# Both of a step's attention-value portions stand in one run at the head of the next step

## The chip, the cores and the metric

The kernel runs on one core of one Trainium2 chip. Its time is the device time of one launch in microseconds (us), lower is better, and the median of several runs counts. One execution was also recorded by the hardware profiler. The engines are PE (TensorE, matrix products), ACT (ScalarE), DVE (VectorE), POOL (GpSimd) and SP (which issues transfers); each works through its own program in order, and they wait for each other by semaphores.

## The reference

Two transformer layers on x of shape (8, 512, 128), float32. Cut to what matters:

```python
x = x + L0_attn(layernorm(x))    # 16 heads of width 8; q and k scaled to unit length,
                                 # out = softmax(g_scale * q k^T) v
x = x + L0_ffn(layernorm(x))     # top 1 of 8 experts, width 32, gelu
x = x + L1_attn(layernorm(x))    # 16 heads of width 64, causal softmax, then w_o
x = L1_ffn(layernorm(x))         # top 2 of 8 experts, width 512, gelu, then layer norm
```

The change concerns the product of the first attention, softmax(...) v, alone; everything it computes stays as it is.

## The kernel before, in words

The work of the eight batches is laid over one long loop of passes `i` from -3 to 8, each of eight steps `p` from 0 to 7 (`steps`). In a pass the stages stand side by side, each for another batch: the second attention of batch i, which works on one pair of heads per step (`o.pair(0)`), the first attention of batch i + 2, the small layers between them (batches i + 1 and i + 3), and the routing of batch i - 1. The dense second expert layer follows after the loop. What follows is about the loop.

The first attention of a batch is cut into 16 portions, one for each group of four heads and each block of 128 keys, and a step has two of them, `o.cosine(0)` and `o.cosine(1)`. For each portion PE computes the scores (`cosines`, L1662, four products of 32 x 128), ACT takes their exponential into one of two buffers (`cosine_exp`, L824, two instructions of 128x1024), and PE multiplies the result with the values (`values0`, L1675, four products that each fill 16 columns). The second attention has, for its pair, score products in three units (`score_unit`, L1529), score products for the maximum in three units for the next pair (`max_unit`, L1498; DVE takes the maxima, L1085), projections of the pair after that (`project`, L1469), the sums (L1559, L1561), the transposed maxima (L1509) and the products with the values (`values1`, L1548).

All score units, of both attentions, alternate between two banks of PSUM, the tile `scores`: a unit may be opened only when the unit two before it has been taken out by ACT or DVE (`unit_open`). In a step the units come as pair 0, max 0, the two halves of portion 0, pair 1, max 1, pair 2, max 2, and the two halves of portion 1; then the next step's pair 0, for which the bank of the first half of portion 1 must be free. The many smaller results alternate in the same way between the two banks of the tile `work` (`work_open`, `work_moved`), in the order that `work_order` writes down.

PE's program is written out by hand at the end of the tensor block: the head of a step is `score_unit(o.g, 0)`, `max_unit(..., 0)`, `values0` and the first half of `values1`, then `cosines` of portion 0. Near the end of a step stands `cosines` of portion 1 and behind it the tail, which depends on p: nothing at p = 0; `group_operands` (L1648, eight transposes into two banks of `work`) at p = 1, 3, 5 and 7; besides that `projection_out` (L1578) at p = 1 and p = 6, `values1_rows` (L1469) at p = 3, the transposes of L1476 at p = 5, `logits0` and `hidden0` (L1596, L1605) at p = 2, and `experts0_out` and `qkv0` (L1637, L1638, L1588) at p = 4. Portions and pairs run together in the six passes i = 0 to 5; in the two passes before them the first attention runs without pairs, and behind them it is over.

Of the kernel before, what the change touches and what calls it, by code (L numbers as in the profile page):

```python
# [217 lines left out]
def layers_kernel(nc, x, wqkv0, g_scale, wg0, s0, bias_ln0, w1_0, b1_0, w2_0, b2_0,  # L218
# [3 lines left out]
    with ctx:  # L222
# [101 lines left out]
        def vstat(h):  # L324
            n = TILES * H0 * VCOLS
            return a0_part(VSTAT + (h % 2) * n, n).rearrange("p (t h d) -> p t h d", t=TILES, h=H0)

        def prob0(c):
            return a0_part(PROB0 + (c % PROB0_SLOTS) * HG * SEQ, HG * SEQ)
# [207 lines left out]
        def unit_done(eng, *unit):  # L537
            eng.wait_ge(score_free[UNIT_NO[unit] % 2], unit_fills(*unit) + 1)
# [915 lines left out]
        def _(pe):  # L1454
# [34 lines left out]
            def max_unit(g, i):  # L1489

                if i == 0:
                    pe.wait_ge(qk1_hi, 2 * g + 2)
                d = unit_open(pe, "max", g, i)
                tiles = (((3, 0),), ((2, 0), (0, 3 * P)), ((1, 0),))[i]
                for n, (qt, at) in enumerate(tiles):
                    width = (qt + 1) * P
                    for j in range(2):
                        last = mm(d[:, j * SEQ + at:j * SEQ + at + width],  # L1498
                                  q_hi[heads(j), g % 2, qt * P:(qt + 1) * P],
                                  k_hi[heads(j), g % 2, 0:width], start=(n == 0),  # L1500
                                  stop=(n == len(tiles) - 1))
                last.then_inc(unit_full("max", g, i), 1)
# [148 lines left out]
            def cosines(c):  # L1651

                s, g, kb = c // STEPS0, c % STEPS0 // TILES, c % TILES
                if kb == 0:
                    work_moved(pe, "qT", s, g)
                    work_moved(pe, "kT", s, g)
                for half in range(2):
                    d = unit_open(pe, "cosine", c, half)
                    for i in range(2):
                        j = 2 * half + i  # L1660
                        rows = slice(STRIP * j, STRIP * (j + 1))
                        last = mm(d[:, i * SEQ:(i + 1) * SEQ],  # L1662
                                  qkT0[rows, 1, g % 2, kb * P:(kb + 1) * P],
                                  qkT0[rows, 0, g % 2, :], start=True, stop=True)
                    last.then_inc(unit_full("cosine", c, half), 1)

            def values0(c):

                s, g, kb = c // STEPS0, c % STEPS0 // TILES, c % TILES
                if kb == 0:  # L1670
                    pe.wait_ge(out_free[1], s * GROUPS0 + g + 1)
                unit_done(pe, "cosine", c, 0)
                unit_done(pe, "cosine", c, 1)
                for j in range(HG):
                    last = mm(outs[STRIP * j:STRIP * j + VCOLS, 1, :],  # L1675
                              vstat(s)[:, kb, g * HG + j, :], prob0(c)[:, j * SEQ:(j + 1) * SEQ],
                              start=(kb == 0), stop=(kb == TILES - 1))
                last.then_inc(out_full[1] if kb == TILES - 1 else pv0_done, 1)
# [34 lines left out]
            for o in steps():  # L1713
# [2 lines left out]
                    score_unit(o.g, 0)  # L1716
                if o.pair(1) is not None:
                    max_unit(o.pair(1), 0)
                if o.cosine(-1) is not None:
                    values0(o.cosine(-1))  # L1720
                if o.pair(-1) is not None:
                    values1(o.pair(-1), (0, 1))
                if o.cosine(0) is not None:
# [67 lines left out]
                    project("k", 1, o.pair(2))  # L1791
                if o.cosine(1) is not None:
                    cosines(o.cosine(1))
                if o.cosine(0) is not None:
                    values0(o.cosine(0))

                if p in (1, 3, 5) and s is not None:
                    group_operands(s, p // 2 + 1)
# [132 lines left out]
```

## Time and profile before

| | us |
|---|---|
| median of 3 runs | 1633.49 |
| lowest, highest run | 1622.28, 1648.9 |
| the profiled execution, its own time | 1636.53 |
| its span, first to last instruction | 1634.8 |
| PE busy | 1327.0 (81%) |
| DVE busy | 934.6 (57%) |
| ACT busy | 851.8 (52%) |
| POOL busy | 600.4 (37%) |
| `values0` on PE (L1675) | 148.4 busy, 1024 records |
| mean granted TensorE clock | 0.917 of full |

The profile page lists busy time by engine, the span in 40 slices, the chain of waits that ended last, and groups of instructions by source line. PE records a float32 product as two instructions, so that the four products of one portion's `values0` are eight records. The timeline lists instructions in order of time, merged where they follow each other from one line; what is in brackets is the engine's idle time before and what ended it. The clock that the throttle granted has two levels in this trace, full (2.4 GHz) and half (1.2 GHz).

### The profile page before, as it was taken

What the parts mean: (1) busy time and instruction counts of PE and PEld (TensorE: products, weight loads), DVE (VectorE), ACT (ScalarE), POOL (GpSimd) and SP (SyncE); (2) the same over time, 40 slices, a digit from 0 to 9 for tenths busy, and PEclk for the clock granted to TensorE, in tenths of its full rate; (3) what the DMA queues carried; (4) which work ended last, traced back from release to release, by engine and by line L of the source; (5) the groups of instructions that cost most, each with busy time, mean ns of one, the idle gap of its engine ahead of it and who ended that gap; (6) DMA issues with size and microseconds to landing.
All of it is one profiled execution on the core that took longest, in us unless ns stands there. A gap on an engine that the chain in (4) does not pass through costs nothing.

```text
span 1634.8 us, 27815 instructions
## 1 busy us (share of the span) xinstructions
PE 1327.0 (81%) x9189; PEld 798.3 (49%) x9189; DVE 934.6 (57%) x3262; ACT 851.8 (52%) x1642; POOL 600.4 (37%) x768
## 2 busy tenths in 40 slices
PE   3878888988888789889988988988888884599970
PEld 1223444554455445545445444544555553488860
DVE  5355755565756576656555764555554654265655
ACT  3665665656565556555654665444424531255533
POOL 1010322233253335333423442235325444265554
PEclk7878999999999999989998999899979987699985
DMA  7060990000000000000000000001010000212222
GB/s 288 1 229 1 8 3 1 1 7 8 1 14 8 7 1 21 1 7 3 19 1 8 8 8 1 7 8 59 8 43 36 1 11 22 90 54 55 58 90 104
DMA packets 63051, 53.17 MB, mean 33 GB/s; under 512 B 39752, under 2 KB 49488, under 8 KB 62656
## 3 DMA queue, kind: packets, MB, share of 16 engines
q1 hardware_dynamic: 58592, 42.47, 13.2%
q0 software_dynamic: 4320, 8.92, 1.6%
q8 instruction: 78, 1.28, 0.3%
q14 instruction: 61, 0.50, 0.1%
HBM read 20.56 MB, written 30.81 MB: 31 GB/s over the span
## 4 chain that ended last, share of the span: by engine, by line
PE 59%; DVE 17%; ACT 14%; issue 7%; POOL 2%; DMA 1%; POOLq 1%; SPq 0%; DVEq 0%; ACTq 0%
PE scores L1529 10%; PE work L1469 8%; PE outs L1675 7%; PE outs L1548 6%; DVE scores L1085 5%; ACT a_buf L824 5%; PE work L1578 4%; PE scores L1498 3%; DVE ra L1078 3%; PE scores L1662 3%; PE work L1561 3%; ACT ra L830 3%; PE outs L1860 2%; ACT rsum L836 2%; PE work L1559 2%
## 5 line engine op out<-in xcount | busy, mean ns | idle before, releaser
L1085 DVE CUSTOM_DVE_ANT_0 scores<-scores,mask_qk 128x512 f32<-128x512 f32 (+3 forms) x512 | 239.3, 520 | 240.8 <-PE scores L1498 238.1
L824 ACT ACTIVATE a_buf<-scores 128x1024 f32<-128x1024 f32 x256 | 248.0, 1026 | 110.7 <-PE scores L1662 101.4
L676 POOL TENSOR_SCALAR_AFFINE_SELECT big<-big 128x256 f32<-128x256 f32 x256 | 100.9, 407 | 541.5 <-ACT big L818 540.7
L818 ACT ACTIVATE big<-scores 128x1024 f32<-128x1024 f32 (+1 forms) x192 | 169.2, 882 | 231.0 <-PE scores L1529 224.5
L1529 PE MATMUL scores<-ra 64*128 64x512 f32 (+3 forms) x1536 | 188.8, 352 | 47.2 <-ACT a_buf L824 33.0
L686 POOL TENSOR_TENSOR big<-big 128x768 f32<-128x768 f32 x64 | 118.6, 1854 | 191.2 <-PE work L1561 191.0
L1529 PEld LDWEIGHTS scores<-ra 64*128 64x128 f32 x1536 | 124.4, 193 | 109.4 <-ACT a_buf L824 42.3
L1548 PE MATMUL outs<-big 128*64 128x512 f32 (+3 forms) x1024 | 164.8, 449 | 2.2 <-DVE yT L1109 2.2
L1675 PE MATMUL outs<-a_buf 128*16 128x512 f32 x1024 | 148.4, 655 | 8.6 <-DVE wqkv_lo L1032 4.9
L1109 DVE TENSOR_TENSOR yT<-outs,rsum 128x512 f32<-128x512 f32 x64 | 44.3, 692 | 148.4 <-ACT rsum L841 148.4
L1548 PEld LDWEIGHTS outs<-big 128*64 128x64 f32 x1024 | 64.2, 137 | 115.9 <-issue 103.4
L973 ACT ACTIVATE big<-scores,b_sb 128x128 f32<-128x128 f32 x284 | 81.1, 368 | 74.8 <-PE scores L1850 43.5
L669 POOL TENSOR_TENSOR rstd<-var_eps,minus_half 128x4 f32<-128x4 f32 x48 | 50.5, 1052 | 161.9 <-DVE var_eps L1047 161.9
L830 ACT CAST ra<-work 128x512 fp32r<-128x512 f32 x128 | 75.0, 586 | 61.7 <-PE work L1469 59.3
L773 POOL DMA_INDIRECT choice_rows<-big x71 | 69.7, 982 | 81.6 <-DVE big L1410 79.7
L1078 DVE TENSOR_TENSOR ra<-work,ra 128x512 fp32r<-128x512 f32 x128 | 87.9, 687 | 18.1 <-ACT ra L830 12.7
L1498 PE MATMUL scores<-ra 64*128 64x512 f32 (+3 forms) x512 | 81.6, 355 | 14.1 <-DVE neg_max L1085 13.1
L836 ACT ACTIVATE rsum<-work 128x512 f32<-128x512 f32 x64 | 38.2, 597 | 101.7 <-PE work L1561 101.7
L1529 PE MATMUL scores<-neg_max_T,pick 64*128 64x512 f32 (+3 forms) x512 | 85.7, 329 | 0.0
L1662 PE MATMUL scores<-qkT 32*128 32x512 f32 x512 | 74.3, 516 | 12.8 <-ACT a_buf L824 10.5
L689 POOL TENSOR_TENSOR big<-big 128x512 f32<-128x512 f32 x64 | 82.4, 1288 | 5.0
L1469 PE MATMUL work<-x_hi,wqkv_hi 128*128 128x512 f32 x128 | 67.7, 529 | 20.0 <-ACT rsum L836 19.8
(216 smaller groups left out, 2600.7 us busy)
## 6 DMA issues: line engine op xcount, KB each, us to landing
sorted_rows<-xrows SPq DMA_DIRECT2D x33, 520.0 KB, 6.8
big<-sorted_rows SPq DMA_DIRECT2D x71, 65.0 KB
a_buf<-in_w SPq DMA_DIRECT2D x2, 2048.0 KB, 8.2
a_buf<-choice_rows SPq DMA_DIRECT2D x16, 256.0 KB, 4.9
a_buf<-in_x SPq DMA_DIRECT2D x8, 256.0 KB, 2.9
x_rows<-x SPq DMA_DIRECT2D x8, 256.0 KB, 2.0
ra<-x_rows SPq DMA_DIRECT2D x8, 256.0 KB
out<-a_buf SPq DMA_DIRECT2D x8, 256.0 KB, 2.0
```

The lines of the kernel that those rows point to most:

```text
L686: nc.gpsimd.tensor_tensor(tsum, prob1(g, 0)[:, :, P:SEQ], prob1(g, 1)[:, :, 0:3 * P], ALU.add).then_inc(tsum_step, 1)
L818: activation(prob1(g, i), d[:, :, 0:256] if i == 2 else d, ACT.Exp, scale=SCALE1).then_inc(unit_free("pair", g, i), 1)
L824: activation(prob0(c)[:, i * 1024:(i + 1) * 1024], unit_wait(act, "cosine", c, i), ACT.Exp).then_inc(unit_free("cosine", c, i), 1)
L830: copy(dst[:, g % 2, :], w).then_inc(qk1_hi, 1)
L1078: v.tensor_tensor(lo[:, g % 2, :], w, hi[:, g % 2, :].bitcast(F32), ALU.subtract).then_inc(free_of(which, g), 1)
L1085: return v.tensor_tensor_reduce(scores_, scores_, mask_qk[:, SEQ - width:SEQ], -1.0, 3e38, ALU.add, ALU.min, neg_max[:, qt, j:j + 1])
L1469: last = mm(dst, a, c, start=(n == 0), stop=(n == 2))
L1498: last = mm(d[:, j * SEQ + at:j * SEQ + at + width], q_hi[heads(j), g % 2, qt * P:(qt + 1) * P], k_hi[heads(j), g % 2, 0:width], start=(n ...
L1529: last = mm(d[:, j * SEQ + at:j * SEQ + at + width], lhs, c[heads(j), g % 2, queries], start=(n == 0 and term == 0), stop=(n == len(blocks ...
L1548: last = mm(outs[heads(j), 0, kb * P:], v1[:, kb, n * D1:(n + 1) * D1], probs, start=(kb == 0), stop=(kb == TILES - 1))
L1662: last = mm(d[:, i * SEQ:(i + 1) * SEQ], qkT0[rows, 1, g % 2, kb * P:(kb + 1) * P], qkT0[rows, 0, g % 2, :], start=True, stop=True)
L1675: last = mm(outs[STRIP * j:STRIP * j + VCOLS, 1, :], vstat(s)[:, kb, g * HG + j, :], prob0(c)[:, j * SEQ:(j + 1) * SEQ], start=(kb == 0), ...
```

## The change

PE's program alone is written differently. Before, portion 0 of a step was multiplied with its values near the end of the same step, behind `cosines` of portion 1, and portion 1 at the head of the next step. Now both stand at the head of the next step, one behind the other. No instruction is added or taken away, and DVE, ACT, POOL and SP have the same programs as before.

```diff
                     score_unit(o.g, 0)
                 if o.pair(1) is not None:
                     max_unit(o.pair(1), 0)
-                if o.cosine(-1) is not None:
-                    values0(o.cosine(-1))
+                for n in (-2, -1):
+                    if o.cosine(n) is not None:
+                        values0(o.cosine(n))
                 if o.pair(-1) is not None:
                     values1(o.pair(-1), (0, 1))
                 if o.cosine(0) is not None:
...
                 if o.cosine(1) is not None:
                     cosines(o.cosine(1))
-                if o.cosine(0) is not None:
-                    values0(o.cosine(0))
 
                 if p in (1, 3, 5) and s is not None:
                     group_operands(s, p // 2 + 1)
```

The first place is PE at the seam between steps p = 0 and p = 1, where a step has no tail. `qkT` are the operands of the first attention, `a_buf` holds its exponentials and values, `ra` the operands of the second attention and `big` its exponentials. Before:

```order
L1469 MATMUL work<-x_hi,wqkv_lo 128x512
L1662 MATMUL scores<-qkT 128x512 x4
L1675 MATMUL outs<-a_buf 16x512 x4
L1529 MATMUL scores<-ra 128x512 x6
L1529 MATMUL scores<-neg_max_T,pick 128x512 x2
L1498 MATMUL scores<-ra 128x512 x2
L1675 MATMUL outs<-a_buf 16x512 x4
L1548 MATMUL outs<-big 64x512 x2
L1548 MATMUL outs<-big 64x384 x2
L1662 MATMUL scores<-qkT 128x512 x4
```

And with the change:

```order
L1469 MATMUL work<-x_hi,wqkv_lo 128x512
L1662 MATMUL scores<-qkT 128x512 x4
L1529 MATMUL scores<-ra 128x512 x6
L1529 MATMUL scores<-neg_max_T,pick 128x512 x2
L1498 MATMUL scores<-ra 128x512 x2
L1675 MATMUL outs<-a_buf 16x512 x8
L1548 MATMUL outs<-big 64x512 x2
L1548 MATMUL outs<-big 64x384 x2
L1662 MATMUL scores<-qkT 128x512 x4
```

The four products that stood between portion 1's scores and the next pair's scores stand behind the maximum's scores now, in one run with the four that were there.

The second place is PE at the seam between p = 4 and p = 5, where the first layer's experts are the tail. The difference, with its context:

```order
 L1662 MATMUL scores<-qkT0 128x512 x4
-L1675 MATMUL outs<-a0_buf 16x512 x4
 L1637 MATMUL work<-w2_0_sb,a0_buf 128x128 x2
 L1638 MATMUL work<-b2_0_sb,a0_buf 128x128
```

```order
 L1529 MATMUL scores<-neg_max_T,pick 128x512 x2
 L1498 MATMUL scores<-ra 128x512 x2
-L1675 MATMUL outs<-a0_buf 16x512 x4
+L1675 MATMUL outs<-a0_buf 16x512 x8
 L1548 MATMUL outs<-big 64x512 x2
```

The tail follows the scores of portion 1 directly, and the head has the run of eight. The seams at the other steps differ in the same way.

## Rows read from the trace of the kernel before

**Rows 1.** The profile page: busy time by engine, the granted clock in 40 slices, the chain.

```profile
PE 1327.0 (81%) x9189; PEld 798.3 (49%) x9189; DVE 934.6 (57%) x3262; ACT 851.8 (52%) x1642; POOL 600.4 (37%) x768
...
PEclk7878999999999999989998999899979987699985
...
PE 59%; DVE 17%; ACT 14%; issue 7%; POOL 2%; DMA 1%; POOLq 1%; SPq 0%; DVEq 0%; ACTq 0%
```

**Rows 2.** Timeline of PE, two projections: start, us, engine, line, tiles [idle before].

```profile
801.39 0.50 PE L1469 MATMUL work<-x_hi,wqkv_hi 128*128 128x512 f32 x1
...
802.19 0.40 PE L1469 MATMUL work<-wqkv_hi,x_hi 128*128 128x512 f32 x1
```

**Rows 3.** Timeline of PE, seam from p = 0 to p = 1.

```profile
806.87 1.05 PE L1675 MATMUL outs<-a_buf 128*16 128x512 f32 x8
808.19 0.98 PE L1529 MATMUL scores<-ra 64*128 64x512 f32 x6 [0.27 <-ACT a_buf L824]
...
809.57 1.05 PE L1675 MATMUL outs<-a_buf 128*16 128x512 f32 x8
810.55 1.73 PE L1548 MATMUL outs<-big 128*64 128x512 f32 x8
812.20 0.50 PE L1662 MATMUL scores<-qkT 32*128 32x512 f32 x4
```

**Rows 4.** Timeline of ACT, the same seam.

```profile
807.02 1.95 ACT L824 ACTIVATE a_buf<-scores 128x1024 f32<-128x1024 f32 x2
```

**Rows 5.** Timeline of PE, seam from p = 1 to p = 2.

```profile
825.29 3.84 PE L1578 MATMUL work<-wo_sb,yT 128*128 128x128 f32 x32 [0.45 <-DVE qkT L1131]
```

**Rows 6.** Timeline of DVE, the same seam.

```profile
823.32 0.68 DVE L1078 TENSOR_TENSOR ra<-work,ra 128x512 fp32r<-128x512 f32 x1
824.54 1.29 DVE L1131 CAST qkT<-work 128x512 fp32r<-128x512 f32 x2 [0.55 <-PE work L1648]
```

**Rows 7.** Timeline of PE, tail of p = 2 and middle of p = 3.

```profile
846.40 1.96 PE L1605 MATMUL work<-a_buf,w1s 128*128 128x512 f32 x4
...
856.67 0.80 PE L1529 MATMUL scores<-ra 64*128 64x384 f32 x6 [3.07 <-ACT a_buf L824]
```

**Rows 8.** Timeline of DVE, tail of p = 2.

```profile
844.84 0.68 DVE L1078 TENSOR_TENSOR ra<-work,ra 128x512 fp32r<-128x512 f32 x1
```

**Rows 9.** Timeline of ACT, step p = 3.

```profile
851.73 1.28 ACT L877 ACT_TABLE_LOAD   x1
...
855.60 1.94 ACT L824 ACTIVATE a_buf<-scores 128x1024 f32<-128x1024 f32 x2
```

**Rows 10.** Timeline of PE, the end of p = 4's tail.

```profile
895.40 1.34 PE L1588 MATMUL work<-wqkv_sb,a_buf 128*128 128x384 f32 x2 [0.26 <-DVE res L1332]
```

**Rows 11.** Timeline of DVE, the same place.

```profile
894.84 0.76 DVE L1332 TENSOR_TENSOR res<-res,work 128x256 f32<-128x256 f32 x2
```

**Rows 12.** Timeline of PE, heads behind the tails of p = 6 and p = 7.

```profile
935.86 0.96 PE L1529 MATMUL scores<-ra 64*128 64x512 f32 x6
...
952.42 0.96 PE L1529 MATMUL scores<-ra 64*128 64x512 f32 x6
```

**Rows 13.** Timeline of DVE, tail of p = 7.

```profile
950.97 0.68 DVE L1078 TENSOR_TENSOR ra<-work,ra 128x512 fp32r<-128x512 f32 x1
```

**Rows 14.** Stretches behind p = 3's long wait: us, busy by engine, clock, DMA.

```profile
227.00:235.00 8.00, 7.33 (x40) 5.50 (x40) 3.07 (x15) 3.83 (x6) 2.16 (x4) 0.59 1.49 2
384.00:392.00 8.00, 6.94 (x52) 5.23 (x48) 4.29 (x17) 3.70 (x6) 2.16 (x4) 0.81 0.00 1
857.00:869.00 12.00, 11.21 (x63) 7.17 (x59) 5.68 (x25) 5.63 (x10) 4.11 (x6) 0.57 0.00 1
```

**Rows 15.** A longer and a shorter wait of PE, in the timeline.

```profile
180.14 0.38 PE L1509 MATMUL work<-ident_b,neg_max_hl 128*128 128x128 bf16 x4 [3.00 <-DVE ra L1078]
...
1044.85 1.03 PE L1694 MATMUL work<-wg_sb,xnT 128*128 128x8 f32 x8 [1.37 <-DVE ra L1078]
```

**Rows 16.** The stretch behind the shorter one, columns as in rows 14.

```profile
1045.00:1050.00 5.00, 4.85 (x27) 2.83 (x27) 0.94 (x3) 1.83 (x4) 2.08 (x2) 0.66 0.00 0
```

## The prediction

> **What bounds the kernel.** I read the page first: PE is busy for 81% of the span, no other engine above 57%, the chain of waits lies on PE for 59% and on DVE and ACT for 31%, and the granted clock is near full in the loop's middle but not everywhere [rows 1]. So PE's own program sets the time, together with the short waits at which it is released by ACT or DVE. The change touches PE's order alone. I therefore went through PE's timeline for the whole pass i = 3 (about 785 to 950 us; it repeats six times with a period of 156 to 160 us), and at each of its eight seams looked at ACT and DVE for what would release PE if it came earlier. A moved instruction costs its time at the new place and gives it back at the old one only if what stands behind it can start earlier; that is the question at each seam.
>
> **The price at the head.** One portion of `values0` takes 0.98 us at full clock: one starts at 809.57 and `values1` behind it at 810.55 [rows 3]. At the head the moved portion joins one that is there already. The first product after another kind of tile lasts longer than one that follows its own kind: a projection's first product has 0.50 us, the first of the next projection, directly behind, 0.40 [rows 2], so 0.1 us more. Before, the portion stood alone between two other kinds; in a run with its twin one such transition falls away, whereas the tail keeps its own. I take 0.87 us for the addition at the head (0.98 less 0.11). The bounds: 0.98 if a run saves nothing, and 0.5 if the two portions' fixed parts merged entirely, for which no row speaks. Nothing absorbs it there: `cosines` starts at 812.20 directly behind `values1`, with no wait [rows 3], and the later waits in the step count from PE's own instructions and move along.
>
> **What comes back at the old place**, seam by seam, for a full pass.
>
> - p = 0, no tail: PE waits already, 0.27 us, for ACT's exponential of the first half, and starts the pair's scores at 808.19 [rows 3]. ACT runs from 807.02 to 808.97 for two halves [rows 4]; the first ends there at 808.0, and no earlier portion of PE changes that. The cover of 0.98 us turns into idle time, 0.27 becomes about 1.25. Returned: 0. Net +0.87.
> - p = 1, 3, 5: the tail is `group_operands`. Its second half needs the `work` bank of `k`, which DVE frees at 824.00 (823.32 + 0.68), and what stands behind waits for DVE's copy that now starts at 824.54 [rows 5, 6]. Without `values0` the first half is done long before 824.00, DVE goes over to the copy at 824.00 at once, 0.54 us earlier, and I count 0.49. Net +0.38, three times: +1.14.
> - p = 2: the hidden layer starts at 846.40 [rows 7] and could start when DVE has freed `k`'s bank, at 845.52 [rows 8]: 0.9 us earlier, and with it the next pair's scores and ACT's exponential of them. In p = 3 PE then waits 3.07 us for ACT, which between loads two tables for the gelu and starts the portion's exponentials at 855.60 [rows 7, 9]. ACT's sequence begins 0.9 us earlier, whereas PE reaches its wait at the same time as before: here the 0.87 at the head costs nothing, since the wait covers it. The wait falls to about 2.2. Net -0.9.
> - p = 4: the tail ends in `qkv0`, which waits 0.26 us until DVE has taken out the experts' first result. DVE does that from 894.84 on [rows 10, 11], at the end of an unbroken row of routing instructions (L1062 to L1209) that doesn't depend on the tail. Returned: 0, the wait becomes 1.2. Net +0.87 in the four passes with both routing and `qkv0`, -0.11 in the first and the last, where one of them is missing.
> - p = 6: the output projection needs nothing that is late, and the head behind it starts without a wait at 935.86 [rows 12]. All of 0.98 returns. Net -0.11.
> - p = 7: as p = 1, with the head directly behind the transposes at 952.42; DVE frees the bank at 951.65 [rows 12, 13], four transposes (0.44) follow, so 952.09. Returned 0.33. Net +0.54.
>
> Sum of a full pass: 0.87 + 1.14 - 0.9 + 0.87 - 0.11 + 0.54 = +2.4 us. Four such passes give 9.6. Pass 0 has 1.6 (p = 1 has no projection behind its transposes, so it goes as p = 7; p = 4 at -0.11). Pass 5 has 2.2 (p = 4 at -0.11; at p = 5 and p = 7 nothing returns, for DVE is late there or the tail is empty). Together **+13.4 us**. In the two passes without pairs the order hardly changes (the portions stood side by side already, with the transposes between them at most), and there ACT's exponentials bind: 0. The part after the loop is untouched.
>
> **The clock.** Behind each of the six waits of 3.07 us the granted clock falls to half for a while: means of 0.59, 0.81 and 0.57 in stretches of 8, 8 and 12 us [rows 14]; two more passes look like the second and one like the third. At half the clock PE does half its work, so a stretch costs its length times the missing share, 3.3, 1.5 and 5.2 us; over the six passes 3.3 + 3 x 1.5 + 2 x 5.2 = 18.2, 3.0 each. With 2.2 us, the wait lies between these (of the same length one, 3.00, kept the clock) and those of 1.0 to 1.5, most of which kept it; but one, 1.37 [rows 15], has 0.66 over the 5 us behind it [rows 16], 1.7 us. I take half of the six as saved: -9.1. Against it stand ten new waits of about 1.2 us, at p = 0 and p = 4, close behind others; I count one drop, +3. Clock: -6.
>
> The Trainium skill (TensorE: Matmul & The Clock Gate, "Why this matters for your kernels") says that long idle gaps between bursts of matmuls send the clock back to its lower rate, and that shorter ones don't. If 2.2 us counts as short in its sense, all 18.2 come back, which is the first rival below; the trace's 3.00 us without a drop shows that the length alone doesn't decide.
>
> **Sum:** 13.4 - 6 = +7 us. Against the profiled execution, 1636.5, that is 1643.5. The median of the runs shown is 3 us lower, so I predict a median of **1640 us**, +0.4%.
>
> **The rivals.**
>
> 1. The clock stays up behind all of p = 3's waits: 13.4 - 18.2 = -5, 1629 us. For it: the wait loses almost a third. Against it: the fall came behind all six so far, whatever the phase, and one came behind 1.37 us. 0.18.
> 2. The dependences alone count, since PE's clock falls as often as before: +13.4, or +19 if the run saves no transition (48 x 0.11 more): 1647 to 1652. For it: no row shows a run of two at full clock. 0.22.
> 3. Slower beyond a doubt: the new waits at p = 0 and p = 4 lose the clock. The place is the head behind them, the price 3.0 us, the mean of the six above. For it: each of the new waits stands some us behind PE's usual short ones, as the 1.37 us did which lost it. Against it: most waits of this length kept the clock. All ten: +30, with the 13.4 together +43, 1677. It passes 2% from seven drops on, with none saved at p = 3. 0.11.
> 4. The run of two is much cheaper than its parts, or PE's tails start so much earlier that ACT and DVE get ahead for good. To pass 2%, 33 us over 48 seams, each would have to bring 0.7 us, and with the 13.4 of dependences 1.0, all that a portion costs. Nothing in the profile says so: 1595. 0.05.
>
> My forecast has the remaining 0.44.
>
> **Range and chances.** Forecast, rivals 1 and 2 hold 0.84 between 1629 and 1652; the median of three runs before lay within 1622 to 1649, so it may be off by some us by itself. 1624 to 1660 holds that and part of rival 3. 2%, 33 us, is about what a measurement of this kernel can tell from no change. Faster by over 2%, below 1601: rival 4, 0.05. Slower by over 2%, above 1666: rival 3, 0.11, with 0.01 for what I haven't seen. Within 2%: 0.83.
>
> **What would show it.** Right: at p = 0's seam PE waits 1.2 to 1.3 us before the pair's scores, for ACT's L824, six times; in p = 3 the wait is 2.1 to 2.3 instead of 3.07; at p = 4 PE waits about 1.2 us before L1588 for DVE; a run of 16 records of L1675 takes 1.8 to 1.9 us from its start to `values1`; a pass without a fall of the clock is about 2.4 us longer. PE's busy time falls by up to 5 us at equal clock. Wrong: if at p = 1, 3 and 5 the full 0.98 us returns, the sum loses 3 x 6 x 0.49 = 9 us and the change is neutral or better; if the tail of p = 2 does not start earlier, 0.9 x 6 = 5 us are added and all of the clock's return is lost; if the clock's mean in the loop falls, rival 3.

## The result, and the profile after

The changed kernel takes 1661.24 us (median of 4 runs, 1656.16 to 1668.99); the kernel before, in the same set, 1640.13. The ratio is 1.021, with an interval from 1.012 to 1.030: slower, by 1 to 3%. Every ratio in this document is taken over the runs of its set that count as fast, here only two of the four of the kernel before, whereas medians, means and clocks are over all runs, so that the two medians alone give 1.013. I had forecast 1640. A second set of runs of the same change gave 1.011 (1.007 to 1.015). Over all sets the mean is 1661 us for the ten runs of the change and 1641 for the 84 runs of the kernel before, so +20 us, 1.2%. The 1633.49 that the prediction started from, a median of three runs, was 8 us lower than that mean.

The profiled execution has 1660.31 us, span 1658.6. The page of after, busy time, clock and chain [rows 1]:

```profile
PE 1332.8 (80%) x9189; PEld 807.1 (49%) x9189; DVE 940.0 (57%) x3262; ACT 852.1 (51%) x1642; POOL 600.0 (36%) x768
...
PEclk7878999999999989998999999989989987699995
...
PE 53%; DVE 18%; ACT 15%; issue 9%; POOL 3%; POOLq 1%; DMA 1%; SPq 0%; DVEq 0%; ACTq 0%
```

PE's share of the chain falls from 59% to 53%, and its busy time is 6 us longer with the same 9189 instructions: the work got neither more nor less, but parts of it ran at half clock, and PE waits more. Its waits sum to 270.8 us instead of 254.2. The six passes i = 0 to 5 (from the first scores of p = 0 to those of the pass behind) take 972.9 us instead of 945.2; what comes ahead is 2.7 us shorter and what comes behind 1.1.

**The seams are as predicted.** The timeline of PE of after, p = 0's seam in pass 3 [rows 3]:

```profile
828.78 0.51 PE L1662 MATMUL scores<-qkT 32*128 32x512 f32 x4
830.55 1.20 PE L1529 MATMUL scores<-ra 64*128 64x512 f32 x6 [1.26 <-ACT a_buf L824]
...
832.53 2.87 PE L1675 MATMUL outs<-a_buf 128*16 128x512 f32 x16
835.33 1.73 PE L1548 MATMUL outs<-big 128*64 128x512 f32 x8
```

The wait went from 0.27 to 1.26 us. But the scores behind it take 1.20 and the run of two portions 2.87: the clock fell here. The same view from p = 1's tail, and from the end of p = 2's tail to the wait in p = 3 [rows 5, 7]:

```profile
848.84 0.53 PE L1648 MATMUL work<-ident_r,parts 128*128 128x128 f32 x4 [0.54 <-DVE ra L1078]
...
870.66 1.96 PE L1605 MATMUL work<-a_buf,w1s 128*128 128x512 f32 x4
...
873.91 1.91 PE L1675 MATMUL outs<-a_buf 128*16 128x512 f32 x16
875.75 1.73 PE L1548 MATMUL outs<-big 128*64 128x512 f32 x8
...
880.93 0.79 PE L1529 MATMUL scores<-ra 64*128 64x384 f32 x6 [2.22 <-ACT a_buf L824]
```

The bank of `k` costs 0.54 us where the portion used to cover it; at full clock the run of two takes 1.84 us to the start of `values1`, which is 2 x 0.98 less 0.12; the long wait is 2.22 instead of 3.07.

**The new cost is in the clock at p = 4.** Steps p = 4 and p = 5 of the passes 1 to 4, one window each, in the kernel before (columns as in [rows 14]):

```profile
397.49:439.78 42.29, 36.59 (x267) 20.51 (x266) 26.00 (x98) 23.00 (x43) 13.29 (x19) 1.00 0.02 8
554.35:596.68 42.33, 36.57 (x267) 20.47 (x266) 26.01 (x99) 23.00 (x43) 13.27 (x19) 1.00 0.02 7
711.23:755.97 44.74, 39.43 (x268) 21.73 (x268) 25.76 (x99) 23.14 (x43) 13.28 (x19) 0.92 0.02 7
872.46:916.32 43.86, 38.10 (x267) 21.11 (x266) 25.33 (x98) 23.00 (x43) 12.27 (x16) 0.96 0.02 7
```

And after:

```profile
399.50:445.45 45.95, 39.46 (x268) 22.09 (x268) 26.36 (x98) 23.04 (x43) 13.83 (x20) 0.93 0.02 7
562.72:612.08 49.36, 43.88 (x267) 24.66 (x266) 26.00 (x99) 23.15 (x43) 13.91 (x20) 0.83 0.02 6
727.67:777.00 49.33, 43.88 (x267) 25.21 (x266) 26.17 (x99) 23.14 (x43) 13.82 (x20) 0.83 0.02 6
894.14:939.96 45.82, 39.50 (x267) 21.74 (x266) 25.99 (x99) 23.05 (x43) 13.91 (x20) 0.93 0.02 7
```

Read the second number of a row (its length) with the clock: 42.3 us at full clock before, and up to 49.4 at 0.83 after; none of the four is at full clock. The sum is 190.5 us instead of 173.2, so +17.2, of which about 1 us per pass is order. Pass 2 of the kernel before has the portion ahead of the tail's small products, all at full clock:

```profile
571.75 1.05 PE L1675 MATMUL outs<-a_buf 128*16 128x512 f32 x8
572.73 0.71 PE L1637 MATMUL work<-w_sb,a_buf 128*128 128x128 f32 x4
573.37 0.48 PE L1638 MATMUL work<-b_sb,a_buf 8*128 8x128 f32 x2
...
577.27 0.89 PE L1588 MATMUL work<-wqkv_sb,a_buf 128*128 128x384 f32 x2 [0.25 <-DVE res L1332]
578.09 0.96 PE L1529 MATMUL scores<-ra 64*128 64x512 f32 x6
```

In pass 2 of after the clock falls ahead of the tail, behind a wait that both kernels have, and this runs at half clock:

```profile
576.91 1.03 PE L1694 MATMUL work<-wg_sb,xnT 128*128 128x8 f32 x8 [1.25 <-DVE ra L1078]
...
579.95 0.79 PE L1469 MATMUL work<-x_hi,wqkv_hi 128*128 128x512 f32 x1
...
582.25 1.22 PE L1637 MATMUL work<-w_sb,a_buf 128*128 128x128 f32 x4
583.40 0.79 PE L1638 MATMUL work<-b_sb,a_buf 8*128 8x128 f32 x2
...
589.75 1.65 PE L1588 MATMUL work<-wqkv_sb,a_buf 128*128 128x384 f32 x2
591.33 1.65 PE L1529 MATMUL scores<-ra 64*128 64x512 f32 x6
...
593.75 2.79 PE L1675 MATMUL outs<-a_buf 128*16 128x512 f32 x16
596.47 1.73 PE L1548 MATMUL outs<-big 128*64 128x512 f32 x8
```

and in pass 4 the same tail at full clock, with the new wait at its end [rows 10]:

```profile
916.79 0.71 PE L1637 MATMUL work<-w_sb,a_buf 128*128 128x128 f32 x4
917.43 0.48 PE L1638 MATMUL work<-b_sb,a_buf 8*128 8x128 f32 x2
918.77 0.89 PE L1588 MATMUL work<-wqkv_sb,a_buf 128*128 128x384 f32 x2 [0.85 <-DVE res L1332]
919.59 1.44 PE L1529 MATMUL scores<-ra 64*128 64x512 f32 x6
```

There are two forms of the loss. In pass 2 the clock was down before the tail, and it stays down through the tail's small products and the next head. In pass 4 the clock was up in the tail, PE waits 0.85 us for DVE, and it falls directly behind. Where the clock was up through all of the step, the new wait has the length that I had forecast; so in pass 3 of e6_p4 (below, moved at p = 4 only), and there too the clock falls in the head behind it:

```profile
744.99 0.89 PE L1588 MATMUL work<-wqkv_sb,a_buf 128*128 128x384 f32 x2 [1.24 <-DVE res L1332]
745.80 1.58 PE L1529 MATMUL scores<-ra 64*128 64x512 f32 x6
```

### The profile page after: what moved, and what is told of

Same layout as the page of the kernel before. It is cut to its first block, busy times and chain, and to the rows that moved or that the text cites. A ratio compares the mean times of both kernels' runs of the same rounds, so it can differ in the third digit from the quotient of the medians.

```text
span 1658.6 us, 27816 instructions
## 1 busy us (share of the span) xinstructions
PE 1332.8 (80%) x9189; PEld 807.1 (49%) x9189; DVE 940.0 (57%) x3262; ACT 852.1 (51%) x1642; POOL 600.0 (36%) x768
## 4 chain that ended last, share of the span: by engine, by line
PE 53%; DVE 18%; ACT 15%; issue 9%; POOL 3%; POOLq 1%; DMA 1%; SPq 0%; DVEq 0%; ACTq 0%
PE scores L1529 10%; PE work L1469 7%; PE outs L1675 7%; PE outs L1548 6%; DVE scores L1085 5%; ACT a_buf L824 5%; PE work L1578 4%; DVE ra L1078 4%; PE scores L1498 3%; PE work L1561 3%; ACT ra L830 3%; ACT rsum L836 2%; PE scores L1662 2%; PE work L1559 2%; PE outs L1859 1%
## 5 line engine op out<-in xcount | busy, mean ns | idle before, releaser
L1529 PE MATMUL scores<-ra 64*128 64x512 f32 (+3 forms) x1536 | 189.6, 353 | 49.0 <-ACT a_buf L824 36.0
L1529 PEld LDWEIGHTS scores<-ra 64*128 64x128 f32 x1536 | 123.5, 192 | 109.1 <-ACT a_buf L824 38.9
L1675 PE MATMUL outs<-a_buf 128*16 128x512 f32 x1024 | 140.9, 670 | 9.8 <-DVE wqkv_lo L1032 6.4
L1498 PE MATMUL scores<-ra 64*128 64x512 f32 (+3 forms) x512 | 82.2, 357 | 16.6 <-DVE neg_max L1085 13.4
L1529 PE MATMUL scores<-neg_max_T,pick 64*128 64x512 f32 (+3 forms) x512 | 86.4, 332 | 0.0
```

Of the source, the lines that this page charges most:

```text
L1498: last = mm(d[:, j * SEQ + at:j * SEQ + at + width], q_hi[heads(j), g % 2, qt * P:(qt + 1) * P], k_hi[heads(j), g % 2, 0:width], start=(n ...
L1529: last = mm(d[:, j * SEQ + at:j * SEQ + at + width], lhs, c[heads(j), g % 2, queries], start=(n == 0 and term == 0), stop=(n == len(blocks ...
L1675: last = mm(outs[STRIP * j:STRIP * j + VCOLS, 1, :], vstat(s)[:, kb, g * HG + j, :], prob0(c)[:, j * SEQ:(j + 1) * SEQ], start=(kb == 0), ...
```

## The experiments

Each kernel was timed in five rounds beside the kernel before. Run times scatter by 1% with the mean granted clock of the run, and do so within every kernel: a common line through the runs of all kernels has 12.1 us (11.3 to 12.9) for each 0.01 of the clock. So beside the ratio stands the difference from before at equal clock (what is left when each run is moved along that line to the mean clock of before), and the part that goes with the clock. The split is rough, as the clock that falls in a wait costs less than one that falls in work.

| kernel | moved at p | runs | median us | ratio (interval) | mean clock | at equal clock | with the clock |
|---|---|---|---|---|---|---|---|
| before | none | 84 | 1641.0 | 1 | 0.9153 | 0 | 0 |
| change, first set | all | 4 | 1661.2 | 1.021 (1.012 to 1.030) | 0.910 | +14.4 ± 2.9 | +6.4 |
| e5_whole | all | 6 | 1659.8 | 1.011 (1.007 to 1.015) | 0.910 | +13.4 ± 2.4 | +6.6 |
| e9_but4 | all but 4 | 8 | 1650.5 | 1.009 (1.005 to 1.012) | 0.918 | +12.9 ± 2.1 | -3.5 |
| e10_but04 | all but 0, 4 | 12 | 1645.0 | 1.006 (1.003 to 1.010) | 0.917 | +7.2 ± 1.8 | -1.7 |
| e3_odd | 1, 3, 5, 7 | 12 | 1647.1 | 1.004 (1.001 to 1.006) | 0.917 | +7.7 ± 1.8 | -1.5 |
| e2_p04 | 0, 4 | 6 | 1665.8 | 1.015 (1.011 to 1.018) | 0.904 | +9.0 ± 2.6 | +13.7 |
| e6_p4 | 4 | 12 | 1646.8 | 1.003 (1.000 to 1.007) | 0.911 | +1.0 ± 1.8 | +4.8 |
| e7_p0 | 0 | 12 | 1646.4 | 1.000 (0.997 to 1.003) | 0.915 | +3.6 ± 1.8 | +0.2 |
| e1_p26 | 2, 6 | 6 | 1624.8 | 0.988 (0.985 to 0.992) | 0.924 | -5.7 ± 2.5 | -10.5 |
| e12_p26 | 2, 6 | 12 | 1628.7 | 0.996 (0.992 to 0.999) | 0.922 | -3.3 ± 1.8 | -7.8 |
| e11_p2 | 2 | 12 | 1628.8 | 0.995 (0.992 to 0.998) | 0.924 | -2.2 ± 1.9 | -10.7 |
| e8_fill | 2, 6 and a fill | 12 | 1646.1 | 1.006 (1.003 to 1.009) | 0.908 | -3.6 ± 1.9 | +8.8 |
| e4_omit | none, two left out | 12 | 1644.9 | 0.997 (0.993 to 1.000) | 0.910 | -4.4 ± 1.8 | +6.6 |

A ratio is taken in its own set of runs; the last two columns use all sets.

**Only p = 2 and p = 6 moved** (e1_p26). The edit, which the other partial kernels share but for the numbers:

```diff
+                if (p - 1) % PAIRS in (2, 6) and o.cosine(-2) is not None:
+                    values0(o.cosine(-2))
                 if o.cosine(-1) is not None:
                     values0(o.cosine(-1))
...
-                if o.cosine(0) is not None:
+                if p not in (2, 6) and o.cosine(0) is not None:
                     values0(o.cosine(0))
```

> Portion 0 is moved to the next step's head only in steps p = 2 and p = 6; in all others it stays at its old place. Theory A (the waits of 1.2 us that the move opens at p = 0 and p = 4 lose the clock, and so does the bare tail of p = 4): the dependences give -0.6 us at p = 2 and 3 together (the wait of 3.07 us falls to 2.2, and the head costs nothing) and -0.12 at p = 6, so -5 us over six passes; the clock behind p = 3's wait falls for 1.7 us instead of 3.0 as in the full change, -5 more: 8 to 14 us faster than before, no new falls at p = 0 and p = 4. Rival B (the clock falls at random, whatever stands at the seams): the dependences alone, -5 us, with falls anywhere. Rival C (the run of two portions itself costs clock or time wherever it stands): 0 to +5 us, with falls behind the runs at p = 3 and p = 7.

Measured: 1624.8 us, 1.2% below the kernel before, and more than theory A had. Part of the change is a gain.

**Only p = 0 and p = 4** (e2_p04).

```diff
-in (2, 6)
+in (0, 4)
```

> The move is made only in steps p = 0 and p = 4. Theory A: dependences +0.85 at p = 0 in six passes and at p = 4 in four, +8.5 us; on top of it the clock, falls at about half of the p = 0 seams and in the middle or tail of most p = 4 steps, 10 to 20 us; and the full wait of 3.07 us at p = 3 stays, with its falls as before. Together 18 to 28 us slower than before, as much as the whole change. Rival B: +8.5 us and no more than by chance. Rival C: a third of what the whole change costs, +7 us, since a third of the runs of two is here, counting the pass-wise +24.

Measured: 1665.8 us, as slow as the whole change, with the lowest clock of all, 0.904. Theory A's 18 to 28 us hold.

**Only the odd steps** (e3_odd).

```diff
-in (2, 6)
+in (1, 3, 5, 7)
```

> The move is made only in steps p = 1, 3, 5 and 7. The seams of the changed kernel at full clock say +0.22 each at p = 1, 3 and 5 and +0.6 at p = 7, 1.3 us a pass, +8 us. Theory A: that, and clock falls as before: +5 to +10 us. Rival C: the runs of two lose the clock here as well, +15 us or more. Rival B: +8 us.

Measured: +7.7 us at equal clock, against 10.1 of the prediction's terms, and no effect on the clock.

**The portion left out** (e4_omit): the kernel before without the first portion's product at p = 0 and p = 4 of the six passes; it isn't done anywhere, so the sum is one portion short. A second edit, in `values0`, lets the portion behind it start the sum instead.

```diff
-                              start=(kb == 0), stop=(kb == TILES - 1))
+                              start=(kb == 0 or kb == 1 and left_out(c)),
+                              stop=(kb == TILES - 1))
...
-                if o.cosine(0) is not None:
+                if not (0 <= o.i <= 5 and p in (0, 4)) and o.cosine(0) is not None:
                     values0(o.cosine(0))
```

> The kernel before, but in the six passes with pairs the first portion's product with the values is left out in steps p = 0 and p = 4 (12 products of four; the output is wrong by them), and nothing is put in its place. Where it stood, PE waits 1.25 us for ACT at p = 0 and about 1 us for DVE at p = 4. By the dependences alone this changes nothing, 0 us (at p = 4 of the first and the last pass, without that wait, -1 us each). Theory A: the waits and the bare tail lose the clock as in the whole change, although there is less work: 8 to 18 us slower, with the seams at p = 0 and p = 4 as uneven as there. Rival B: -2 to 0 us.

Measured: 1644.9 us, no change, though 12 x 0.98 us of work are gone. Windows of steps p = 4 and p = 5 in its passes 2 and 3:

```profile
555.72:603.96 48.24, 42.93 (x259) 24.29 (x258) 25.75 (x99) 23.16 (x43) 13.32 (x19) 0.82 0.02 6
719.97:769.09 49.12, 44.03 (x261) 25.53 (x260) 25.74 (x99) 23.15 (x43) 13.29 (x19) 0.79 0.02 6
```

With less to do PE is busy for 44.0 us here; the kernel before has 36.6 in its passes at full clock. So the loss at p = 4 needs no run of two and nothing added at the head: it is enough that the portion is missing from the tail. (With the portion goes its cover of the wait for DVE, so the run does not tell the two apart.) That it would cost 8 us or more in all, as I expected in one case, did not come.

**The whole change again** (e5_whole), in another set of runs, with no edit to the changed kernel.

> The changed kernel as it is, timed again for more executions. Over 24 runs of the kernel before its time follows its mean granted clock, 12.4 us for each 0.01; by that line the four runs of the changed kernel stand 14 us above the kernel before at an equal clock, and 4 us more by a lower clock (0.910 against 0.913). Theory A': the dependences are 11 to 14 us (the three parts run so far sum to 5.4 less, 8.6 and 7.7 more, +11), and the clock falls by 0.003 to 0.006 in the mean, so 15 to 21 us slower. Rival: the clock part was chance, and at an equal clock only the dependences stay, 11 to 14.

Measured: 1659.8 us. The clock is again 0.910.

**Only p = 4** (e6_p4) **and only p = 0** (e7_p0).

```diff
-in (2, 6)
+in (4,)
```

> The move is made in step p = 4 only. Moving at p = 0 and p = 4 together gave +8.6 us at an equal clock and lowered the clock by 0.009, 12 us. Dependences here: +0.87 in four passes, -0.1 in two, +3.3 us. Theory D (the clock is lost at p = 4: the tail there is 8 products of 128 columns, and the portion of 512-column products that stood ahead of it is gone): the clock falls by 0.006 to 0.009, 7 to 11 us more, 10 to 14 together. Theory E (it is lost by the waits of 1.2 us, of which p = 0 has six and p = 4 four): 4 to 5 us by the clock, 8 together.

```diff
-in (2, 6)
+in (0,)
```

> The move is made in step p = 0 only. Dependences: +0.85 in six passes, +5.1 us. Theory D: the clock hardly changes, 0 to 3 us more, 5 to 8 together. Theory E: 7 us by the clock, 12 together.

Measured: 1646.8 and 1646.4 us, both within 0.4% of before by the ratios in their set. p = 4 alone lowers the clock by 0.004, p = 0 alone doesn't. That speaks against theory E; but p = 4's fall is smaller than the 0.006 to 0.009 of theory D. Windows of steps 4 and 5 of e6_p4, passes 1 and 3:

```profile
396.13:445.27 49.14, 43.83 (x268) 24.51 (x267) 25.84 (x98) 23.15 (x43) 13.21 (x19) 0.83 0.02 6
722.05:766.81 44.76, 37.98 (x267) 21.23 (x266) 25.96 (x99) 23.01 (x43) 13.31 (x19) 0.96 0.02 7
```

Its four passes are at 0.83, 0.86, 0.96 and 0.93. Both together (e2_p04) have more than the sum of the two, 22.7 us above the mean of before against 9.6; their clocks differ by more than p = 4's own part, and why is open.

**The wait of p = 3 filled** (e8_fill): e1_p26, with one block of `values1_rows` and the projection of q put ahead of the waiting scores of p = 3, from behind them.

Both stand no longer at their old places further on in the step (not shown):

```diff
+                if p == 3 and l1 is not None:
+                    values1_rows(l1, 2, 1)
+                if p == 3 and o.pair(2) is not None:
+                    project("q", 0, o.pair(2))
                 if o.pair(0) is not None:
                     score_unit(o.g, 1)
```

> The portion is moved at p = 2 and p = 6 only, as in the run that was 19 us faster; besides, in step p = 3 the projections of v (block 2) and of q, 0.7 us each, are issued ahead of the second pair unit instead of behind it, so that they fill the wait for ACT's gelu, which is 2.2 us there. Dependences: 1.5 us less in each of seven passes, -10 us against that run, -16 against the kernel before. If long waits of PE are what costs the clock, the mean clock rises above that run's 0.924, and it is 25 to 35 us faster than before. If it is not, 16 to 29.

Measured: 1646.1 us, 17 to 21 us above the two medians of what it was built on; both expectations missed. The timeline of PE, pass 1:

```profile
385.37 0.80 PE L1529 MATMUL scores<-ra 64*128 64x384 f32 x6 [0.63 <-ACT a_buf L824]
...
387.86 0.62 PE L1529 MATMUL scores<-ra 64*128 64x256 f32 x6 [0.83 <-ACT big L818]
...
391.31 0.59 PE L1613 MATMUL work<-ident_b,a_buf 128*8 128x128 bf16 x4 [1.58 <-DVE ra L1078]
...
396.81 1.91 PE L1675 MATMUL outs<-a_buf 128*16 128x512 f32 x8
```

The wait of 2.22 us is down to 0.63, and the clock stays up behind it. But the projection had covered two other waits: 0.83 us stands 2.5 us further on (not there in e1_p26, whose timeline has the scores directly behind the projection), and 1.58 where e1_p26 has 0.64. There the clock falls (the window 390 to 392 us has 0.62; in e1_p26 it fell between 386 and 388), and the portion at 396.81 has 1.91 us instead of 1.05. PE's waits sum to 252.8 us in the trace, 251.1 in e1_p26. The hole was moved, not filled; at equal clock the kernel is as fast as e1_p26, and its clock is lower by 0.015. What of this comes from where the waits now lie, I can't say.

**The change without p = 4** (e9_but4) **and without p = 0 and 4** (e10_but04).

```diff
-in (2, 6)
+in (0, 1, 2, 3, 5, 6, 7)
```

> The whole change, except that at p=4 the first portion stays where the kernel before has it. Theory A (the change costs what the order on TensorE costs, about 13.5 us at equal granted clock, of which p=4 is 5.2; and the granted clock falls behind the new wait of 0.85 us at p=4, which stretches the small products of that step's end): the sum at equal clock falls to about +8, the granted clock comes back to that of the kernel before (0.914), the stretch between p=4's tail and the next scores takes 9.1 us again in most passes instead of 11 to 15: 1645 to 1653. Theory B (the lower clock belongs to the moves together, by p=0's wait or by the longer runs of 16x512 products, not to p=4): the clock stays at 0.910 and p=4's stretch stays long: 1653 to 1658.

```diff
-in (2, 6)
+in (1, 2, 3, 5, 6, 7)
```

> The whole change except at p=0 and p=4: moved at p=1, 2, 3, 5, 6 and 7. By the terms of the prediction (+10.1 for the four odd steps, -6.1 for p=2 and 6) the order gives +4; by the parts timed so far +7.9 and -5.2, so +2.7, and the clock is that of the kernel before or a little above it, as 2 and 6 alone had 0.924: 1637 to 1648 (theory A). Theory B (all moves add up through the clock too: -17.3 for 2 and 6 and +5 for the odd ones as timed): 1630 to 1636. If neither holds and the steps' costs don't add, 1650 or more.

Measured: 1650.5 and 1645.0 us. Leaving p = 4 alone brings the clock from 0.910 back to 0.918 and takes 10 us off. The windows of steps 4 and 5 in e9_but4, passes 1 to 4:

```profile
397.72:440.22 42.50, 36.64 (x268) 20.63 (x268) 26.43 (x98) 23.02 (x43) 13.85 (x20) 1.00 0.02 7
558.36:600.91 42.55, 36.63 (x268) 20.63 (x267) 26.27 (x99) 23.02 (x43) 13.95 (x20) 1.00 0.02 7
719.04:762.82 43.78, 38.11 (x267) 20.89 (x267) 26.22 (x99) 23.11 (x43) 13.94 (x20) 0.96 0.02 7
879.61:923.39 43.78, 38.10 (x268) 21.00 (x268) 26.10 (x99) 23.11 (x43) 13.94 (x20) 0.96 0.02 7
```

The lengths of before are back, in a kernel that has every other portion moved: theory A's time and clock hold, theory B falls. e9_but4's part at equal clock, +12.9, is above the +8 expected; e10_but04's +7.2 is above the +2.7. The pieces do not add up to within their errors at equal clock, so single pieces of 1 to 4 us in that column aren't to be trusted further than that.

**Only p = 2** (e11_p2), **and p = 2 and 6 once more** (e12_p26).

```diff
-in (2, 6)
+in (2,)
```

> Moved at p=2 only. The wait of 3.07 us of step 3's head becomes 2.2 in six passes, so 6 x 0.98 = 5.9 less at equal clock, since the run of two saves 0.11 there too and the tail of p=2 hides nothing. Theory A (shorter wait, and with it a clock that stays up more often): 1626 to 1634. Theory B (2 and 6 alone had a high clock by chance or by p=6): 1634 to 1639. If the gain of 2 and 6 were p=6's alone: 1641 to 1645.

The last has no edit against e1_p26.

> The kernel moved at p=2 and 6 only, once more, in another set of runs. If its granted clock of 0.924 is its own: 1621 to 1629. If that clock was chance, and only the order gains (5.2 us at equal clock): 1633 to 1639.

Measured: 1628.8 and 1628.7 us. The high clock of e1_p26 is its own (0.922 in the second set), and it comes from p = 2. Windows of step 3 of e11_p2, passes 1, 2 and 3:

```profile
373.57:394.71 21.14, 16.89 (x130) 8.91 (x130) 12.84 (x50) 15.26 (x26) 7.50 (x9) 1.00 0.00 2
528.62:552.06 23.44, 19.67 (x130) 11.08 (x130) 12.85 (x50) 15.36 (x26) 7.54 (x9) 0.85 0.00 1
687.35:708.50 21.15, 16.90 (x131) 8.92 (x130) 12.85 (x50) 15.26 (x26) 7.51 (x9) 1.00 0.00 1
```

In three passes of six the clock does not fall at all behind the wait of 2.2 us. Over all kernels it fell behind each of the 36 waits of 3.07 us, and behind 32 of the 42 of 2.2: e11_p2 is, with e10_but04, the best of seven traces, not the typical one. Moving at p = 2 alone is the smallest edit that beats both kernels, the one before by 0.2 to 0.8%; p = 6 adds nothing that can be told.

## Why the prediction was wrong

**The order was right.** The length of each step at full clock, passes 1 to 4, from the starts of L1529 at the heads in the trace of after or, where none of its steps was at full clock, as noted:

| step | before | changed | measured | predicted |
|---|---|---|---|---|
| p = 0 | 16.12 | 16.98 | +0.86 | +0.87 |
| p = 1 | 20.87 | 21.08 | +0.21 | +0.38 |
| p = 2 | 19.23 | 19.35 | +0.12 | 0 |
| p = 3 (both at clock 0.92) | 22.25 | 21.58 | -0.67 | -0.49 |
| p = 4 (e9_but4, same head) | 23.72 | 24.56 | +0.84 | +0.87 |
| p = 5 (e5_whole) | 18.59 | 18.80 | +0.21 | +0.38 |
| p = 6 | 19.54 | 19.43 | -0.11 | -0.11 |
| p = 7 | 16.56 | 17.17 | +0.61 | +0.54 |

(The predicted column sorts the prediction's terms by the step in which they fall: the head gives +0.87 to every step but p = 3, where the wait covers it, and the tail gives back what the prediction says.) The sum is +2.1 us for a full pass instead of +2.4, so about +12 for the six instead of +13.4; the fits at equal clock have +13 to +14. p = 1, 3 and 5 give back 0.65 instead of 0.49, p = 2 0.75 instead of 0.87, p = 7 0.26 instead of 0.33. For p = 4's own portion e6_p4 and e2_p04 have the answer at full clock: step 4 as before (23.75), step 5 19.45 instead of 18.59, so 0.86 and nothing returned. The 0.11 us that a run of two saves is there. The Trainium skill (TensorEngine Tiling (Array Packing), "Tiling Modes") says that a change of tiling mode drains TensorE, without a figure; a run of 16-column products with one such change less shows 0.12, which agrees, though no run here shows that a drain is what it saves.

**The clock term failed: -6 predicted, +6 to +15 measured.** It had two parts, which I read again as missing clock (length times one less the granted clock, summed over the six passes; a microsecond missing in a wait costs nothing, so it is a bound on the time lost):

- Step 3. I counted half of 18.2 us as saved. The trace of after has 8.8 us missing there, before 18.8; but e5_whole, with the same program, has 15.4. Over the seven traces with p = 2 moved (e8_fill left aside) the mean is 13.6, over the six without 18.2. So a quarter comes back in the mean, not half; single traces spread so far (8.5 to 20.5 and 11.9 to 25.6) that the quarter itself is uncertain. The Trainium skill (TensorE: Matmul & The Clock Gate, "What's actually happening") says that the chip watches TensorE's activity in a rhythm of its own, which doesn't follow the program, so that the clock's changes can come at another place from one run to the next. The traces agree: with one and the same program, steps 4 and 5 of pass 3 took 49.3 us in the trace of after and 43.6 in that of e5_whole.
- The new waits. I counted ten of them as one fall, +3 us, and named more as rival 3, at a chance of 0.11. Steps 4 and 5 have 28.3 us missing after (e5_whole 26.3), before 7.8, and steps 0 to 2 have 10.0 (6.8), before 0. Together that is 30 us more of missing clock in the trace of after, from which the 10 of step 3 go off. e9_but4, where the part of steps 4 and 5 is back at 7.1, shows that the larger part is p = 4's alone.

The step of the prediction that failed is thus "I count one drop, +3", with its ground, "most waits of this length kept the clock". ("I take half of the six as saved" was too much as well, by some 4 us.) It treated the wait at p = 4 as one of ten alike, and looked at its length only. The traces show that the length does not decide. At p = 0's seam, where products of 512 columns stand ahead of the wait, the clock fell behind 11 of 32 waits of 1.25 us (those of the six kernels that have them, but for four at which it was down already). Behind the waits of p = 4, 0.85 to 1.24 us at the end of a row of small products, it fell in 8 of 8.

That is one form of the loss. The other is that a fall which begins ahead of p = 4's tail lasts. Falls begin there in kernels of both kinds. In passes 1 to 4 of the five kernels without the portion in the tail (the change, e5_whole, e2_p04, e6_p4, e4_omit) 16 of 20 passes have one, and 9 of these last 13.7 us or more. In the nine kernels with it 19 of 36 passes have one, and 2 last so long (e8_fill, e12_p26). By both forms together the head of p = 5 runs wholly or partly at half clock in 17 of 20 passes without the portion, and in 4 of 36 with it.

That the portion's absence from p = 4's tail does this is shown, by e4_omit and e9_but4. Why is argued only: the portion was the one dense stretch there, 0.98 us between a place where the clock often falls and a row of small products. Taking it away removes dense work and opens a wait, and no run has the one without the other. A long stretch costs more than I priced as well: 49.14 us against 43.2 at full clock with p = 4 moved (42.3 + 0.86), so 5.9 us, twice the 3.0 of the rival. In the trace of after there are further falls around p = 0's seam (three of six passes, in one of them from before the wait) and in p = 2 (two passes), most of them about 1.6 us.

So rival 3's mechanism came true in part: regularly at p = 4, in about a third of the seams at p = 0. I had priced it only with all ten waits, at +43 with the order, and left out the case in which one of the two places falls regularly.

**Where the 20 us went.** In the runs: about 12 to 14 order, about 6 to 8 clock. In the two traces the loop's passes are 27.6 us longer: 12 order, the rest clock, at p = 4 and 5 about +13 (17.2 less 1.06 x 4), at p = 0 to 2 about +9, at p = 3 about -6. The two traces are single executions and scatter: the part behind the loop, the same program in all kernels, has between 60 and 74 us of missing clock.

**The base.** The prediction took the median of three runs as 3 us below the trace's; over 84 runs the mean is 4.5 us above the trace. By that alone the same sum gives 1648, and with the clock at zero 1654. So of the 21 us between the forecast and the median measured, about 8 are the base, the rest the clock term, and the order term, +13.4, was right.

## What to carry to other kernels

Price a moved instruction at both ends: the head takes its full time, and the tail gives back only what the next dependence allows; done seam by seam from one trace this held to 0.3 us per pass. Then ask separately what the moved work was for the clock: here dense work ahead of small products and a wait kept TensorE's clock up in most passes, and taking it away cost up to 5.9 us in a pass for one portion of 0.98. Move only where a longer wait stands behind to absorb it: the one place of eight that had such a wait, p = 2, gained 11 us alone in its set: 2 to 5 by the order (2.2 by the line at equal clock, 6 x 0.75 by the length of the step), the rest with the clock.

## What the runs showed of the hardware

- The length of a wait does not tell whether it costs the clock. It fell behind all 36 waits of 3.07 us at p = 3 and behind 32 of 42 of 2.2 us at the same place, behind 11 of 32 of 1.25 us at p = 0's seam, and behind all 8 of 0.85 to 1.24 us at the end of p = 4's small products. A wait of 3.00 us elsewhere kept it [rows 15].
- Small products do not bring the clock back quickly: in pass 2 of after, eight groups of L1637 and L1638 ran one behind the other at half clock (1.22 and 0.79 us instead of 0.71 and 0.48), with PE busy without a break, and the clock rose only within the next head's long run, 17 us after it fell.
- Run-to-run scatter of this kernel on one core is the clock: 1619.7 to 1633.8 us in e11_p2 with 0.928 and 0.921, about 12 us per 0.01 in all kernels. Two versions that differ by less than 1% need the clock beside the time.
- Less work can be no faster: with 12 us of products left out (e4_omit) the time was the same; at the two places PE waits for ACT and DVE instead, and the mean clock is 0.005 lower.
